# Where the maximum jobs stand among a body's fifteen groups: ten doubles, four singles, one double

## What is computed

```python
q, k = _fq_sym(q, axis=-1), _fq_sym(k, axis=-1)
v = _fq_sym(v, axis=2)
attn = jnp.einsum('bhqd,bhkd->bhqk', q, k)
attn = jax.nn.softmax(attn.astype(jnp.float32), axis=-1)
attn = _fq_unsigned(attn, axis=-1)      # scale: row maximum / 255
out = jnp.einsum('bhqk,bhkd->bhqd', attn, v)
```

## Time and profile before

| | before |
|---|---|
| median of the runs | 8865.77 us (8865.53 to 8866.54) |
| profiled execution | 8868.33 us, of this span 8866.5 us |
| PE busy | 8204.1 us (93%) |
| DVE busy | 6557.1 us (74%) |
| ACT busy | 5411.8 us (61%) |
| POOL busy | 5204.3 us (59%) |
| reductions of jobs (L1166) | 4992, 5655.3 us |
| granted PE clock, mean | 0.952 |

### The profile page before, as it was taken

The page is one execution under the profiler, slowest core; times in us unless marked ns, Lnnn a source line. Parts: engine busy times, 40 slices in busy tenths (PEclk is TensorE's granted clock), DMA queues, the critical chain, the costliest instruction groups (busy, mean ns, idle before and its releaser), DMA issues.

```text
span 8866.5 us, 223893 instructions
## 1 busy us (share of the span) xinstructions
PE 8204.1 (93%) x60312; PEld 2566.4 (29%) x60312; DVE 6557.1 (74%) x6161; ACT 5411.8 (61%) x12138; POOL 5204.3 (59%) x3573
## 2 busy tenths in 40 slices
PE   8934899999999999999999999999999999988588
PEld 4510222222222222222222222222222222222343
DVE  8969877777777777777777777777777777710466
ACT  2300576767676767676767676767667676777233
POOL 5724465656565656565656565656656565666356
PEclk9955899999999999999999999999999999999789
DMA  5663002020202020202020202010111111010100
GB/s 162 209 136 114 14 13 33 12 34 12 35 11 34 12 34 12 34 12 34 12 34 12 34 11 34 12 28 19 26 20 25 21 22 24 18 24 7 26 4 4
DMA packets 305414, 303.94 MB, mean 34 GB/s; under 512 B 50718, under 2 KB 297802, under 8 KB 300458
## 3 DMA queue, kind: packets, MB, share of 16 engines
q1 hardware_dynamic: 304682, 303.13, 15.6%
q10 hardware_dynamic: 672, 0.16, 0.0%
HBM read 226.31 MB, written 76.71 MB: 34 GB/s over the span
## 4 chain that ended last, share of the span: by engine, by line
PE 84%; DVE 6%; issue 5%; POOL 2%; ACT 1%; DMA 1%; SPq 0%; DVEq 0%; ACTq 0%; POOLq 0%
PE psum L1378 30%; PE psum L1347 26%; PE psum L1303 15%; PE psum L1357 6%; DVE mpart L1166 3%; PE psum L1268 2%; ACT y L1065 1%; POOL mix L411 1%; PE psum L671 1%; PE psum L1337 1%; DVE act_c L551 1%; PE psum L1405 1%; POOL kq L924 1%; POOL kq L931 1%; PE psum L644 0%
## 5 line engine op out<-in xcount | busy, mean ns | idle before, releaser
L1166 DVE TENSOR_REDUCE mpart<-psum 128x978 f32 x4992 | 5655.3, 1172 | 1414.0 <-PE psum L1303 1341.0
L1065 ACT ACTIVATE y<-psum 128x400 f32<-128x400 f32 x11520 | 5007.0, 506 | 2063.2 <-PE psum L1378 1971.0
L985 POOL TENSOR_SCALAR xh<-y 128x1600 f16<-128x1600 f32 x2880 | 4397.9, 1527 | 2747.2 <-PE psum L1357 1554.1
L1378 PE MATMUL psum<-QT,K 99*128 x11520 | 3180.6, 341 | 68.3 <-ACT y L1065 55.7
L1347 PE MATMUL psum<-y,ones 128*17 128x400 f32 x23048 | 2537.3, 507 | 0.0
L1303 PE MATMUL psum<-K,QS 48*128 48x489 bf16 x9984 | 1768.6, 390 | 288.5 <-DVE mpart L1166 194.0
L1378 PEld LDWEIGHTS psum<-QT,K 99*128 x11520 | 875.6, 97 | 2618.2 <-issue 2477.0
L1357 PE MATMUL psum<-xh,vwin 128*16 128x400 f16 x11528 | 1019.2, 335 | 0.7 <-POOL xh L985 0.7
L1303 PEld LDWEIGHTS psum<-K,QS 48*128 48x128 bf16 x9984 | 433.4, 93 | 1553.6 <-issue 1074.7
L1347 PEld LDWEIGHTS psum<-y,ones 128*17 128x17 f32 x23048 | 401.7, 95 | 651.6 <-ACT y L1065 386.0
L1357 PEld LDWEIGHTS psum<-xh,vwin 128*16 128x16 f16 x11528 | 321.8, 90 | 624.9 <-issue 397.9
(11 more groups left out here) (180 smaller groups left out, 2153.6 us busy)
## 6 DMA issues: line engine op xcount, KB each, us to landing
K<-kT_parts SPq DMA_DIRECT2D x204, 240.0 KB, 8.3
vwin<-v_int SPq DMA_DIRECT2D x579, 80.0 KB, 1.9
K<-kT_parts SPq DMA_DIRECT2D x772, 45.8 KB
kT_parts<-part SPq DMA_DIRECT2D x135, 256.0 KB, 3.3
K<-kT_parts SPq DMA_DIRECT2D x102, 242.0 KB, 8.3
src<-in_ctx_dram SPq DMA_DIRECT2D x46, 512.0 KB, 4.6
v_float<-kv SPq DMA_DIRECT2D x45, 512.0 KB, 5.2
vin<-v_float SPq DMA_DIRECT2D x9, 2560.0 KB, 12.7
```

Source lines behind the costliest of these rows:

```text
L985: pool.tensor_scalar(xh[:, g % YR, :, :], y[:, g % YR, :, :], INT_STEP, 0.0, ALU.mult, ALU.add)\
L1065: act.activation(y[:, s % YR, j, :], s2_bank(GT * s + j), ACT.Exp).then_inc(exp_done, 1)
L1166: dve.tensor_reduce(mpart[:, t, ds(2 * cp + j, 1)], s1_buf(n)[:, :, 0:CHALF], AX.XY, ALU.max)\
L1378: pe.matmul(s2_bank(t), K3[0:MROW, h % 2, ds(c * REGION + t * P, P)], queries, start=True, stop=True).then_inc(s2_ready, 1)
```

## The change

The groups' jobs are laid out anew: s = 0 to 9 have two jobs in a row, s = 10 to 13 one, s = 14 two. No group is split any more. Before, s = 2, 6, 10, 14 had one job, s = 1, 4, 8, 12 two that were split, and the others two in a row. The block turn-out moves from s = 6 to s = 13. `sum_group` no longer has a wait of its own. A body still has 26 jobs, and all other instructions are the same.

```diff
-SINGLE = (2, 6, 10, 14)
-JOBS_AT = [1 if s in SINGLE else 2 for s in range(GROUPS)]
-SPLIT = (1, 4, 8, 12)
+JOBS_AT = [2] * 10 + [1] * 4 + [2]
...
-EPI_SLOT = 6
+EPI_SLOT = 13
...
-            def sum_group(T, g, start):
-                if g >= 0:
-                    pe.wait_ge(exp_done, S2_RING + T + GT * (g + 1))
+            def sum_group(g, start):
...
-                    next_jobs(1 if s in SPLIT else JOBS_AT[s])
+                    next_jobs(JOBS_AT[s])
                     score_tile(s, 2)
                     score_tile(s, 3)
-                    if s in SPLIT:
-                        next_jobs(1)
```

More of the change, by code:

```diff
@@ L1406, in body @@
                             .then_inc(summed_x, 1)
-                        sum_group(T, 0, True)
+                        sum_group(0, True)
                     if later or g != 0:
-                        sum_group(T, g, False)
+                        sum_group(g, False)
                     g = s - LAG_PV
@@ L1434, in _ @@
             for g in range(-LAG_SUM, 0):
-                sum_group(0, g, False)
+                sum_group(g, False)
             for g in range(-LAG_PV, 0):
```

## The result

The changed kernel takes 8953.12 us (median; 8952.05 to 8955.69) against 8865.92 for the kernel before in the same measurement (one run more than in the table ahead of the prediction): a ratio of 1.0097 (95% interval 1.0084 to 1.0109), 87 us slower. The forecast was 8955. The profiled execution after took 8952.05 us, its span 8950.2 against 8866.5, so the trace has to account for 83.7 us.

The account below looks back on a forecast made before the run. TensorE was taken to bound the kernel (84% of the chain), in a buffer loop with VectorE. Per head 3.04 + 2.1 + .8 = +5.9 us, fifteen heads +89: 8866 + 89 = 8955 us, range 8895 to 8995.

Parts of the forecast that it names:

- eight later bodies: Bodies after a block's first: 36.96 us each against 36.58, +.38 (+.18 to +.58), eight in a head +3.04 us.
- first bodies of the last three blocks: First body of each later block in a head: some +.7 us each, mostly +.72 at s = 2; +2.1 a head.
- first body of a head: Opening body of a head's first block: the hold at s = 2 shrinks to about .25 us, taken as 0.
- seam: Between two heads: last reduction ends later, +1.01 us, less .2 back from the half-clock stretch: +.8 a head.
- The loop: TensorE and VectorE: buffer back at 2.84 us, wanted at 2.59; two pairs of jobs take at least 5.01 instead of 4.76.
- the first rival: VectorE returns the second buffer within 2.59 us, so every pair of jobs is free: 8670 us, faster; chance .07.
- Single groups: Groups with one job in later bodies: 2.32 us each, four in a body.
- Turn-out: Block turn-out moved from s = 6 to s = 13, behind a single job before and after: costs 0.
- The wait ahead of the sums: Removed wait for the last exponential of the group before, already fulfilled when reached: 0 taken, bounds 0 to 27 us off.
- Clock: Rival: TensorE's short idles bring one more half-clock stretch per head, some 4 us each: 9015 us; chance .04.

## Why the prediction was right, and where its parts were not

| per head, us | forecast | measured |
|---|---|---|
| eight later bodies, 36.96 forecast, 36.97 measured, each + .38 and + .39 | 3.04 | 3.10 |
| lone tile's wait at the end of a block (3 x) | 0 | .35 |
| first bodies of the last three blocks (3 x) | 2.1 | 1.78 |
| first body of a head | 0 | .15 |
| seam | .8 | .15 |
| sum | 5.9 | 5.5 |

Fifteen heads make 82.3 us; 1.3 in the last head, 1.2 ahead of the first block and 1.1 less behind the last make the 83.7 us of the spans.

- *The loop.* A buffer comes back 2.84 us after the pair's first job, so two pairs can't follow in less than 5.01. After, they take 5.05 to 5.09, and the held groups alternate with free ones: 2.67, 2.39, 2.67, 2.39 and so on (2.67 against 2.68 forecast). With short reductions all of it goes. Here the step held, and with it the answer to the first rival: the split saves nothing in a row of pairs, because what it costs is hidden in the same loop.
- *Single groups.* s = 10 to 13 stay at 2.32, as forecast.
- *First body.* s = 0 was held not at all (2.57 against 2.55; forecast .10), since the lone tile's stretch gives VectorE enough time; s = 1 was held .28 instead of .15 (1.96 us). s = 2 came out at 4.21 us against 4.32. PE's timeline after, the counterpart of the earlier trace rows, from s = 1 to s = 4:

```profile
2915.93 0.51 PE L1374 MATMUL psum<-QT,K 99*128 x2
2916.37 0.87 PE L1301 MATMUL psum<-K,QS 48*128 48x489 bf16 x4
...
2917.89 0.64 PE L1374 MATMUL psum<-QT,K 99*128 x2
...
2918.46 0.38 PE L1301 MATMUL psum<-K,QS 48*128 48x489 bf16 x2
2919.22 0.38 PE L1301 MATMUL psum<-K,QS 48*128 48x489 bf16 x2 [0.37 <-DVE mpart L1164]
...
2922.09 0.51 PE L1374 MATMUL psum<-QT,K 99*128 x2
```

  The second job of s = 2 starts 2.85 us after the first job of s = 1 (2916.37 to 2919.22), the 2.84 of the prediction. It follows the first job of its own group by .76 instead of the .21 of a free pair: held .55, not .79. The .24 less had been lost ahead of it: s = 1 took .12 more than forecast, and the score pair that opens s = 2 .12 more (.57 against .45). The score pair behind the jobs takes .44 as forecast (2919.53 to 2919.97). A first body is .59 us longer, not .70.
- *Turn-out.* "Same instructions, same wait: 0" was wrong in what it was compared with. The turn-out itself costs the same behind a single job at either place, but its pause is worth a hold among pairs: .27 a body by the run with the turn-out left at the seventh group. No term of the sum is off by it, since the three holds of the new place were counted among the groups; what was wrong is that the move itself was said to be free.
- *Lone tile.* A term that was not in the sum. A body that ends in a pair reaches its last exponential later, and the lone tile behind it needs the bank that this frees. The kernel after at a block's end, PE and, last, ScalarE, and then ScalarE in the kernel before:

```profile
3026.03 0.36 PE L1353 MATMUL psum<-xh,vwin 128*16 128x400 f16 x4
3026.62 0.34 PE L1386 MATMUL psum<-QT,K 99*128 x1 [0.23 <-issue]
...
3024.32 1.86 ACT L1063 ACTIVATE y<-psum 128x400 f32<-128x400 f32 x4 [0.63 <-PE psum L1374]
```

```profile
2998.34 1.69 ACT L1065 ACTIVATE y<-psum 128x400 f32<-128x400 f32 x4 [0.55 <-PE psum L1378]
```

  In both kernels the tile starts .43 to .44 after the last exponential, which ends at 3000.03 before (tile at 3000.46) and at 3026.18 after. Behind the start of the value products it stands .59 where it stood .47 (2999.99 before): .115 a block.
- *Seam.* The reductions end 1.08 later, but the maxima's chain no longer meets GpSimd, and the next head starts only .2 later (9.24 to 9.45 us after s = 14). The term of .8 was .65 too high: the maxima's chain behind the last reduction was taken as a fixed length, and a step of 1.07 us in it was a collision that the later start avoids. The prediction's sign of seams a microsecond longer did not come. The misses of seam and later blocks' first bodies (-.65 and -.3) and of lone tile and a head's first body (+.35 and +.15) have opposite signs, so it is in part luck that the total is so near.
- *The wait ahead of the sums.* 0 in the old layout, within the -11 to +6 us that the interval of the run without it leaves.
- *Clock.* No further stretch at half clock: 1.00 in the middle of the head, and one stretch at each of the fifteen seams in both kernels, 6.8 or 10.2 us long. The Trainium skill, page "TensorE: Matmul & The Clock Gate", section "A second HAM failure mode: psum-queue depth-cycling", tells of a kernel in which micro-idles between groups of matmuls made the clock swing; this trace, with 3.8 us of idle time in 190, shows no such swing.

What stays open: the .15 in the first body of a head, and why edits of the seam and of the order of jobs in some heads lengthen the stretch at half clock.

## What to carry to other kernels

Before two operations are moved together, compare the time from the first of them to the return of its buffer with the spacing that the new order asks for; where the second is shorter, the saved gap comes back as a wait. A layout with short pauses between pairs isn't waste if a second engine catches up in them, and a step that pauses anyway belongs where that engine is behind. To see whether an order is bound by such a loop, shorten the other engine's work alone: here that turned a loss of 87 us into a gain of 155.

## What the runs showed that was not expected

- A step of VectorE on 13 columns takes .17 us or waits until GpSimd's operation ends (1.07 for a product of two SBUF inputs, .87 for a scalar step from SBUF to SBUF); with its inputs in PSUM it takes .18 beside the same GpSimd operation. The Trainium skill, page "SBUF — State Buffer", section "Who interferes with whom", says that VectorE and GpSimd share a pair of ports under an exclusive lock, and names steps with two SBUF inputs and the two-port modes as those that need it; the trace agrees for the two inputs, with the 1.07. The .87 was a wait too, but no run shows in which mode that step ran.
- An address from two loop registers costs TensorE's later bodies .40 us each in the old layout (36.59 to 36.18), 47 us in the whole kernel; one register computed once a body gives it back.
- A loop that was written out brought 11.49 MB of instructions instead of .33 and a stop of 3.37 us at a block's end: 190 us slower, although the later bodies themselves were .40 us shorter.
- A shorter pause at the seam isn't always a shorter head. With .19 us less of it (one product in PSUM), the fifteen heads of the profiled execution took 6861.4 us against 6859.6: most first bodies of a head took 40.2 to 41.2 us, every sixth 44.2, behind a stretch at half clock of 17 us instead of 10. With .87 less (the whole chain in PSUM), which should bring 13 us, the fifteen heads of the profiled execution were 14.5 us shorter and the medians 10 (interval 2 to 18), though two of its heads opened behind such a stretch of 17 us.
